# Row factors carried to all partitions by DMA in ten of sixteen graphs, an ELU without a GpSimd pass, and loads split over two queues

## The chip, the core and the metric

The kernel runs on one core of one Trainium2 chip. What counts is the device time of one execution in microseconds. Before the change it is 1097.34 us (median of 3 runs, 1097.25 to 1097.4).

## The reference

Sixteen graphs of 512 nodes with 128 features share one adjacency matrix. Four layers follow each other. Each adds its result to its input and normalises the rows (mean and variance over 128 features).

```python
# x: (16, 512, 128), adj: (512, 512)
# layer 0: 4 heads of 32
scores = where(adj == 0, -inf, q @ k.T / sqrt(32));  o = softmax(scores) @ v
x = layernorm(x + o @ wo.T + bo)
# layer 1: one head
e = leaky_relu(s1[:, None] + s2[None, :], 0.2);  a = softmax(masked e);  x = layernorm(x + a @ (x @ W))
# layer 2: 8 heads of 16, the same kind of scores, a prior of adj, then @ W_out.T
# layer 3
r = relu(x @ w1 + b1)                                  # 256 wide
z = elu(elu(softmax(leaky scores, unmasked) @ (r @ W_fc))) + r
r = relu(z @ w2 + b2)                                  # 128 wide
y = relu(elu(elu(softmax(masked leaky scores) @ (r @ W_hand))) + r)
x = layernorm(x + y)
```

A leaky score of a source i and a target j makes exp(leaky(s_i + d_j)), which is the larger of two products of a factor of i and a factor of j. So the kernel needs, for each target tile, the 512 source factors as a row that stands on all 128 partitions, and the two target factors as one number per partition.

## The kernel before, in words

The nodes of a graph stand as 4 chunks (`C`) of 128 partitions. Every engine works through its own written-out list of stages (`ORDER`, read by `turns`), two characters for each entry: the stage's letter and the graph. Part k of a stage is its k-th appearance. The lists interleave the layers of several graphs, up to four at a time. Which of the eight PSUM banks a stage uses is a list too (`BANK_OF_USE`). All engines, and SyncE's list of DMAs too, work strictly in this order, and semaphores tie them together.

The stages that the change touches:

- **Row factors of layers 1, 3 and 3b** (3b is the second attention of layer 3). ScalarE makes `R`, 128x4, one source factor per node (`exps`). TensorE transposes each column, broadcast to 128 wide, into a bank (`spread_sources`, L569, 4 instructions), and VectorE reads the bank four times: `masked_weights` (L1114) for layers 1 and 3b, `weights` (L1130) for layer 3.
- **Layer 0's reciprocals.** `l0_rcp` makes 128x16 reciprocals; `l0_rd` (L531, 16 matmuls of 32 columns of weights) spreads them into a bank, each head on its 32 partitions; `l0_o` (L1044) multiplies.
- **Layer 2's rows** go by DMA already, in all graphs. VectorE transposes 32x32 blocks of `R2` (`l2_turn`, L1194), SyncE writes them to a line in HBM with 4 DMAs (`l2_rows`, L432) and reads each head's line back with a broadcast to 128 partitions (`l2_spread`, L439) into one of five buffers `row`. VectorE reads a row four times (`l2_p`, L1207).
- **ELU.** After the attention of layer 3, ScalarE writes the quotient v (`l3_v`, L847); GpSimd makes min(v, 0) in pieces of 128x128 (`below_zero`, L1370); ScalarE takes exp twice (L864, L870), and VectorE puts the result together (L1238, L1249). The same holds for 3b (L856).
- **The start.** SyncE issues nine DMAs of projections, then adj as one transfer (L399), then all the later weights (`late_loads`), then x of graph 0 (L423). TensorE runs 12 matmuls that nobody reads (`WARM_UP`, L453), turns five weights (L457, L458) and goes on with x.
- **Fillers.** An entry Z (`keep_warm`, L697) is two matmuls that nobody reads, written into the bank of the next stage. There are 102 of them, 204 matmuls; each fp32 matmul is two instructions in the trace.

## Time and profile before

| | us |
|---|---|
| median of 3 runs | 1097.34 |
| the profiled execution | 1097.66 |
| its span | 1095.9 |
| TensorE busy (PE) | 1028.9 |
| VectorE busy (DVE) | 925.4 |
| ScalarE busy (ACT) | 727.9 |
| GpSimd busy (POOL) | 376.2 |

The span is the profiled execution from its first to its last instruction, and lies 1.8 us below that execution's own time. Busy time is the union of an engine's instructions, so a group's busy time divided by its count is less than the mean duration of one of them, since they overlap in the pipeline. PEld is the loading of weights into TensorE, beside its matmuls. The page's rows for the engines give shares of the span; the stretches further down show where in the span an engine is full.

### The profile page before, as it was taken

What the parts mean: (1) busy time and instruction counts of PE and PEld (TensorE: products, weight loads), DVE (VectorE), ACT (ScalarE), POOL (GpSimd) and SP (SyncE); (2) the same over time, 40 slices, a digit from 0 to 9 for tenths busy, and PEclk for the clock granted to TensorE, in tenths of its full rate; (3) what the DMA queues carried; (4) which work ended last, traced back from release to release, by engine and by line L of the source; (5) the groups of instructions that cost most, each with busy time, mean ns of one, the idle gap of its engine ahead of it and who ended that gap; (6) DMA issues with size and microseconds to landing.
All of it is one profiled execution on the core that took longest, in us unless ns stands there. A gap on an engine that the chain in (4) does not pass through costs nothing. (4 is left out here: it accounts for less than half of the span.)

```text
span 1095.9 us, 26875 instructions
## 1 busy us (share of the span) xinstructions
PE 1028.9 (94%) x9253; PEld 770.6 (70%) x9253; DVE 925.4 (84%) x2533; ACT 727.9 (66%) x1901; POOL 376.2 (34%) x781
## 2 busy tenths in 40 slices
PE   4899989999999999999999999999999999889895
PEld 3576657777777776867777777768677778576785
DVE  2757999999899989899998999998999988877342
ACT  1797776766767777786767677777867663543522
POOL 1013413432525243343325252443433264341322
PEclk6999999999999999999999999999999999999999
DMA  5001110202020210102020201102020202020000
GB/s 125 2 11 60 54 56 20 70 20 78 22 69 21 69 32 32 58 21 79 21 76 23 69 21 65 35 30 60 21 79 11 78 13 68 12 78 20 10 1 20
DMA packets 30997, 46.82 MB, mean 43 GB/s; under 512 B 7824, under 2 KB 10128, under 8 KB 30736
## 3 DMA queue, kind: packets, MB, share of 16 engines
q1 hardware_dynamic: 30864, 45.11, 13.2%
q8 instruction: 76, 1.25, 0.5%
q14 instruction: 57, 0.47, 0.1%
HBM read 40.64 MB, written 4.46 MB: 41 GB/s over the span
## 5 line engine op out<-in xcount | busy, mean ns | idle before, releaser
L1207 DVE SCALAR_TENSOR_TENSOR P<-row,t2e,mask_t 128x512 f32<-128x512 f32 x512 | 358.6, 761 | 7.9 <-PE bank L605 7.0
L751 ACT ACTIVATE probs<-probs,neg_max 128x512 f32<-128x512 f32 x256 | 186.1, 729 | 16.6 <-DVE neg_max L1024 15.9
L1016 DVE CUSTOM_DVE_ANT_0 probs<-bank,mask_add 128x512 f32<-128x512 f32 x256 | 168.0, 682 | 28.7 <-PE bank L502 28.3
L761 ACT ACTIVATE probs_t<-bank 128x512 f32<-128x512 f32 x256 | 151.2, 620 | 4.5 <-PE bank L510 4.2
L510 PE MATMUL bank<-ident,probs 128*128 128x128 f32 x1024 | 144.0, 277 | 7.4 <-ACT probs L751 6.3
L510 PEld LDWEIGHTS bank<-ident,probs 128*128 128x128 f32 x1024 | 113.8, 141 | 36.9 <-ACT probs L751 25.1
L796 ACT ACTIVATE x<-x,shift_l,rstd_l 128x128 f32<-128x128 f32 x256 | 105.0, 484 | 44.7 <-POOL shift_l L1343 44.7
L1361 POOL TENSOR_TENSOR t<-t 128x128 f32<-128x128 f32 x128 | 48.7, 412 | 204.3 <-ACT t L788 204.3
L605 PE MATMUL bank<-P,GH 128*32 128x512 f32 x1024 | 116.2, 594 | 1.9 <-DVE P L1207 1.2
L650 PE MATMUL bank<-t,l_P 128*128 128x257 f32 x512 | 115.1, 383 | 1.1 <-DVE l_P L1130 1.1
L1370 POOL TENSOR_SCALAR e<-v 128x128 f32<-128x128 f32 x128 | 74.8, 611 | 113.6 <-ACT v L847 113.6
L650 PEld LDWEIGHTS bank<-t,l_P 128*128 128x128 f32 x512 | 95.9, 190 | 16.4 <-issue 2.2
L1328 POOL TENSOR_TENSOR rstd_l<-mv_l,ln_eps 128x4 f32<-128x4 f32 x64 | 16.5, 258 | 192.7 <-DVE mv_l L1070 192.6
L605 PEld LDWEIGHTS bank<-P,GH 128*32 128x32 f32 x1024 | 31.2, 110 | 68.2 <-issue 66.3
L1336 POOL TENSOR_TENSOR rstd_l<-rstd_l,neg_half 128x4 f32<-128x4 f32 x64 | 75.0, 1173 | 3.0
L1320 POOL TENSOR_TENSOR x_in<-x_in,bias_o 128x128 f32<-128x128 f32 x64 | 30.3, 505 | 132.9 <-PE bank L473 132.9
L502 PE MATMUL bank<-head_k,head_q 32*128 32x512 f32 x512 | 72.4, 638 | 1.8 <-DVE l_P L1114 0.9
L521 PE MATMUL bank<-probs_t,v 128*32 128x128 f32 x2048 | 70.0, 278 | 0.9 <-ACT probs_t L761 0.7
L521 PEld LDWEIGHTS bank<-probs_t,v 128*32 128x32 f32 x2048 | 52.6, 110 | 19.8 <-issue 12.0
L733 ACT ACTIVATE xTl<-bank 128x512 f32<-128x512 f32 x64 | 38.1, 595 | 40.6 <-PE bank L473 40.4
L581 PE MATMUL bank<-t,l3b_P 128*128 128x129 f32 x512 | 62.3, 277 | 0.5 <-DVE l3b_P L1114 0.5
L581 PE MATMUL bank<-t,l_P 128*128 128x129 f32 x512 | 61.1, 278 | 0.0
(168 smaller groups left out, 2016.3 us busy)
## 6 DMA issues: line engine op xcount, KB each, us to landing
row<-line SPq DMA_DIRECT2D x128, 256.0 KB, 3.5
x_in<-in_x SPq DMA_DIRECT2D x16, 256.0 KB, 2.6
out<-x SPq DMA_DIRECT2D x16, 256.0 KB, 2.1
l_P<-in_adj SPq DMA_DIRECT2D x1, 1024.0 KB, 7.5
line<-turned SPq DMA_DIRECT2D x64, 4.0 KB, 1.4
w_fc<-in_L_gnn_W_fc SPq DMA_DIRECT2D x1, 256.0 KB, 3.0
P<-in_L_gnn_a_fc SPq DMA_DIRECT2D x1, 256.0 KB, 3.6
w_cat<-in_L_gnn_W SPq DMA_DIRECT2D x2, 64.0 KB, 5.9
```

What stands on the lines that cost most here:

```text
L510: last = pe.transpose(ps[:, j * P:(j + 1) * P], probs[m // HEADS0 % 2][:, m % HEADS0, j * P:(j + 1) * P], ident[:, :])
L521: last = pe.matmul(ps[DH0 * h:DH0 * (h + 1), 0:P], g.of(v0)[:, j, DH0 * h:DH0 * (h + 1)], probs_t[c % 2][:, h, j, :], start=(j == 0), stop ...
L581: last = pe.matmul(ps[:, c * (D + 1):(c + 1) * (D + 1)], gat[n]["P"][:, j, (2 * k + c) * P:(2 * k + c + 1) * P], g.of(t)[:, j, 2:3 + D], s ...
L605: last = pe.matmul(ps[DH0 * h:DH0 * (h + 1), :], g.of(GH)[:, j, (GROUP2 * q + h) * W2:(GROUP2 * q + h) * W2 + DH0], P2[:, h, j, :], start= ...
L650: last = pe.matmul(ps[:, 0:HID + 1], gat["l3"]["P"][:, j, c * P:(c + 1) * P], g.of(t3)[:, j, 2:3 + HID], start=(j == 0), stop=(j == C - 1))
L751: act.activation(e, e, ACT.Exp, bias=neg_max[:, m:m + 1], scale=SCALE0, accum_out=g.of(den0)[:, m:m + 1])\
L761: act.activation(probs_t[c % 2][:, h, :, :].rearrange("p j n -> p (j n)"), ps("l0_t", g, m)[:, :], ACT.Copy)\
L796: last = act.activation(y[:, c, :], y[:, c, :], ACT.Identity, bias=shift[n][:, c:c + 1], scale=rstd[n][:, c:c + 1])
L1016: dve.tensor_tensor_reduce(probs[c % 2][:, h, :], ps("l0_s", g, m)[:, :], mask_add[:, c, :], 1.0, -3.0e38, ALU.add, ALU.max, row_max[:, m: ...
L1207: last = dve.scalar_tensor_tensor(P2[:, h % GROUP2, j, :], row(g, h)[:, :], g.of(t2e)[:, j, h:h + 1], mask_t[:, j, :], ALU.max, ALU.mult)
L1336: pool.tensor_tensor(rstd[n][:, :], rstd[n][:, :], neg_half[:, :], ALU.pow)\
L1370: last = pool.tensor_scalar(e[:, c, q:q + P], v(g)[:, c, q:q + P], 0.0, None, ALU.min)
```

## The change

1. **Rows by DMA in graphs 2 to 11** (`ROWS_BY_DMA = range(2, 12)`). For layers 1, 3 and 3b the four columns of `R` are turned on VectorE (`turn`), written to HBM with one DMA (`lay_out`) and read back with a broadcast (`spread`) into a `row` buffer, from which VectorE reads them. Layer 0's reciprocals go the same way (`l0_spread`). In the other six graphs TensorE spreads them as before. Layer 2's lines are written with one DMA where it was four. There are six row buffers where there were five, and which transfer goes to which buffer is a list (`ROW_OF_USE`).
2. **The companion.** A column of ones stands beside the features, and gives the softmax's sum. Beside it now stands a column of its negative, so that the reciprocal yields 1/sum and -1/sum (258 columns for 257, 130 for 129). ScalarE reads the bank twice: v = o/sum, and e = relu(-o/sum). The first exp takes scale -1. GpSimd's pass is gone.
3. **Loads.** ScalarE's queue issues wq, wk, both biases, wv and bias_v; SyncE issues adj in four transfers, the first at once, then x of graph 0, then the later weights. wo, w_out and bias_o come later and are turned later (`out_T`). `WARM_UP` is 4.
4. All lists are written anew. Fillers: 82, that is 164 matmuls.

The core of the diff, long lists left out:

```diff
-ROWS = 5
+ROWS = 6
-WARM_UP = 12
+WARM_UP = 4
+ROWS_BY_DMA = range(2, 12)
 ...
+            def lay_out(n, turned):
+                def f(g, k):
+                    sp.wait_ge(*(sig if n == "l2" else dma_sig)(n + "_turned", g, 1))
 ...
+                    sp.dma_start(g.of(line[n]).rearrange("r (q s) -> q r s", s=BLOCK),
+                                 turned[:, :]).then_inc(signal[n + "_rows"], 16)
+            def free_row(stage, g, k):
+                r, _, last = row_use[stage, k, g.i]
+                if last:
+                    sp.wait_ge(*row_read(last[0], last[2], last[1]))
+                return rows[r], row_filled[r]
+            def spread(n):
+                def f(g, k):
+                    if k == 0:
+                        sp.wait_ge(*(sig if n == "l2" else dma_sig)(n + "_rows", g, 16))
+                    to, done = free_row(n + "_spread", g, k)
+                    sp.dma_start(to[:, :], g.of(line[n])[k * C:(k + 1) * C, :].rearrange("c p -> (c p)")
+                                 .rearrange("(o n) -> o n", o=1).broadcast_to([P, N_NODES])).then_inc(done, 16)
 ...
-                    made = dve.tensor_scalar(q["P"][:, j, :], ps(n + "_s", g)[:, :], q["g"][:, j:j + 1], q["b"][:, j:j + 1],
+                    made = dve.tensor_scalar(q["P"][:, j, :], sources(n, g), q["g"][:, j:j + 1], q["b"][:, j:j + 1],
 ...
+                o, q = ps("l3_o", g, c)[:, 0:HID], gat["l3"]["rden"]
+                act.activation(v3[:, c, :], o, ACT.Copy, scale=q[:, c, 0:1])
+                act.activation(e3[:, c, :], o, ACT.Relu, scale=q[:, c, 1:2]).then_inc(emptied("l3_o", g, c), 1)
```

**Three places in the lists.** On SyncE at the start, before: the projections are first, and x of graph 0 comes after all of the late loads.

```order
L393 DMA bias_q<-in_L0_gnn_bq 128x1
L394 DMA bias_k<-in_L0_gnn_bk 128x1
L395 DMA bias_v<-in_L0_gnn_bv 128x128
L396 DMA bias_o<-in_L0_gnn_bo 128x128
L399 DMA l1_P<-in_adj 128x2048
L403 DMA w1_cat<-in_L1_gnn_W 128x128
L404 DMA P2<-in_L1_gnn_a 128x256
```

After, on the same engine, ahead of and behind the late loads:

```order
L441 DMA l1_P<-in_adj 128x512
L465 DMA x_in_0<-in_x 128x512
L445 DMA w1_cat<-in_L1_gnn_W 128x128
L446 DMA P2<-in_L1_gnn_a 128x256
...
L460 DMA P2<-in_L3_gnn_a_hand 128x256
L441 DMA l1_P<-in_adj 128x512
L465 DMA x_in_1<-in_x 128x512
L435 DMA l3b_P<-in_L0_gnn_wo 128x128
```

x of graph 0 moved from behind the late loads to second place; the second quarter of adj stands behind them.

On SyncE around layer 2 of graph 3, before: a line is written in four pieces and its heads follow one another.

```order
L423 DMA x_in_0<-in_x 128x512
L432 DMA line2_1<-turned2 32x32 x4
L439 DMA row2<-line2_0 128x512
L439 DMA row3<-line2_1 128x512
L439 DMA row4<-line2_1 128x512
L439 DMA row0<-line2_1 128x512
```

After, in the same region: lines and rows of layer 0 and layer 1 of other graphs stand between the heads of layer 2.

```order
L465 DMA x_in_0<-in_x 128x512
L476 DMA l2_line1<-turned2 4x32x32
L491 DMA row3<-l2_line1 128x512
L476 DMA l0_line1<-turned0 4x32x32
L498 DMA row1<-l0_line1 128x1x512
L491 DMA row0<-l2_line1 128x512
L491 DMA row4<-l2_line1 128x512
L476 DMA l1_line0<-l1_turned 4x32x32
L491 DMA row2<-l1_line0 128x512
```

A transfer of one layer now waits in the same queue behind the waits of another layer.

On TensorE at the very end, before: the last graph's layer 3 and 3b with the fillers between them.

```order
L697 MATMUL bank<-ones,ident 128x128 x32
L659 MATMUL bank<-ident,v 128x128 x8
L697 MATMUL bank<-ones,ident 128x128 x2
L674 MATMUL bank<-ident,out_t 128x128 x4
L667 MATMUL bank<-h_t,w3b 128x512 x2
...
L697 MATMUL bank<-ones,ident 128x128 x12
L581 MATMUL bank<-t_0,l3b_P 128x129 x16
L697 MATMUL bank<-ones,ident 128x128 x26
L674 MATMUL bank<-ident,out_t 128x128 x4
```

After, the same stages:

```order
L771 MATMUL bank<-ones,ident 128x128 x14
L732 MATMUL bank<-ident,v 128x128 x8
L747 MATMUL bank<-ident,out_t 128x128 x4
L740 MATMUL bank<-h_t,w3b 128x512 x2
...
L771 MATMUL bank<-ones,ident 128x128 x12
L654 MATMUL bank<-t_0,l3b_P 128x130 x16
L771 MATMUL bank<-ones,ident 128x128 x14
L747 MATMUL bank<-ident,out_t 128x128 x4
```

Behind the last attention product of layer 0 the list of before has 192 filler matmuls, that of after 108.

## Rows read from the trace of the kernel before

**Rows 1.** The page, part 1: busy us (share) and instructions of each engine.
```profile
PE 1028.9 (94%) x9253; PEld 770.6 (70%) x9253; DVE 925.4 (84%) x2533; ACT 727.9 (66%) x1901; POOL 376.2 (34%) x781
```
**Rows 2.** Stretches: length, then busy us of PE, PEld, DVE, ACT, POOL; PEclk, DMA.
```profile
300.00:400.00 100.00, 99.24 (x911) 75.53 (x910) 93.36 (x250) 74.40 (x201) 35.34 (x76) 1.00 0.15 49
...
1060.00:1080.00 20.00, 17.37 (x134) 15.10 (x134) 9.45 (x23) 7.47 (x16) 5.25 (x13) 1.00 0.04 14
```
**Rows 3.** Timeline of SyncE's queue: start us, us; loads of x, seven periods apart.
```profile
346.98 0.33 SPq L423 DMA_DIRECT2D x_in<-in_x  x1
...
769.42 0.33 SPq L423 DMA_DIRECT2D x_in<-in_x  x1
```
**Rows 4.** Groups by line, TensorE: busy us, mean ns, idle before.
```profile
L650 PE MATMUL bank<-t,l_P 128*128 128x257 f32 x512 | 115.1, 383 | 1.1 <-DVE l_P L1130 1.1
...
L697 PE MATMUL bank<-ones,ident 128*128 128x128 f32 x408 | 50.0, 275 | 1.5 <-ACT head_q L741 0.8 <-ACT mask_t L718 0.7
...
L569 PE MATMUL bank<-ident,l_R 128*128 128x128 f32 x128 | 19.7, 279 | 1.1 <-ACT l_g L788 0.9
...
L531 PE MATMUL bank<-ident,rden 128*32 128x128 f32 x512 | 16.9, 273 | 0.0
```
**Rows 5.** Timeline of the start: start us, us, engine.
```profile
4.47 0.43 SPq L396 DMA_DIRECT2D bias_o<-in_L_gnn_bo  x1
...
10.00 1.12 PE L457 MATMUL bank<-ident,l3b_P 128*128 128x128 f32 x4 [3.26 <-DMA bias_o<-in_L_gnn_bo]
...
15.66 0.91 SPq L423 DMA_DIRECT2D x_in<-in_x  x2
...
20.20 1.09 PE L473 MATMUL bank<-ident,x_in 128*128 128x128 f32 x4 [8.87 <-DMA x_in<-in_x]
21.33 0.60 ACT L733 ACTIVATE xTl<-bank 128x512 f32<-128x512 f32 x1 [8.94 <-PE bank L473]
...
29.04 0.69 DVE L1016 CUSTOM_DVE_ANT_0 probs<-bank,mask_add 128x512 f32<-128x512 f32 x1
```
**Rows 6.** Timeline of the end: ELU of the last graph.
```profile
1055.52 0.47 ACT L847 ACTIVATE v<-bank,l_rden 128x256 f32<-128x256 f32 x1 [1.26 <-DVE l_rden L1233]
1056.27 3.96 POOL L1370 TENSOR_SCALAR e<-v 128x128 f32<-128x128 f32 x8 [13.43 <-ACT v L847]
...
1060.26 1.06 ACT L864 ACTIVATE e<-e 128x1024 f32<-128x1024 f32 x1 [2.33 <-POOL e L1370]
...
1081.00 0.62 ACT L856 ACTIVATE x<-bank,l3b_rden 128x128 f32<-128x128 f32 x2 [1.16 <-DVE l3b_rden L1141]
1081.77 2.00 POOL L1370 TENSOR_SCALAR e<-x 128x128 f32<-128x128 f32 x4 [6.89 <-issue]
1083.81 0.63 ACT L864 ACTIVATE e<-e 128x512 f32<-128x512 f32 x1 [2.18 <-POOL e L1370]
```
**Rows 7.** Groups by line, VectorE.
```profile
L1207 DVE SCALAR_TENSOR_TENSOR P<-row,t2e,mask_t 128x512 f32<-128x512 f32 x512 | 358.6, 761 | 7.9 <-PE bank L605 7.0 <-DMA row<-line 0.2
...
L1130 DVE TENSOR_SCALAR l_P<-bank,l_g,l_b 128x512 f32<-128x512 f32 x64 | 50.7, 795 | 0.1
...
L1114 DVE SCALAR_TENSOR_TENSOR l_P<-bank,l_b,mask_t 128x512 f32<-128x512 f32 x64 | 46.4, 739 | 2.0 <-PE bank L569 2.0
...
L1194 DVE STREAM_TRANSPOSE turned<-R 128x32 f32<-128x32 f32 x16 | 3.2, 199 | 0.0
...
L941 DVE TENSOR_SCALAR l_P<-l_P 128x512 f32<-128x512 int32 x4 | 2.2, 609 | 0.0
```
**Rows 8.** Timeline of VectorE and SyncE's queue: graph 0's layer 2 rows.
```profile
100.11 0.21 DVE L1194 STREAM_TRANSPOSE turned<-R 128x32 f32<-128x32 f32 x1
...
100.35 1.74 SPq L432 DMA_DIRECT2D line<-turned  x4
...
103.11 6.63 SPq L439 DMA_DIRECT2D row<-line  x6
...
106.66 2.73 DVE L1207 SCALAR_TENSOR_TENSOR P<-row,t2e,mask_t 128x512 f32<-128x512 f32 x4
```

More of the change, by code:

```diff
@@ L205, in bank_uses, with row_uses @@
     return used
+def row_uses():
+    used, transfers, last, at = {}, [0] * ROWS, [None] * ROWS, 0
+    for name, g, k in turns("sp"):
+        if name.endswith("_spread"):
+            r = int(ROW_OF_USE[at])
+            at += 1
+            transfers[r] += 1
+            used[name, k, g.i] = r, transfers[r], last[r]
+            last[r] = name, k, g
+    return used
 def build_program(nc, x, adj, w, out):
     use = bank_uses()
+    row_use = row_uses()
     with ExitStack() as ctx:
@@ L321, in build_program @@
         for n in GATS:
-            for what, k in (("c4", 1), ("dd", 2), ("b", 3)):
+            for what, k in (("c4", 1), ("dd", 2), ("b", 3), ("turned", 1), ("p", 1)):
                 sem(f"{n}_{what}", k)
@@ L326, in build_program @@
         for n in ("l3", "l3b"):
-            for what in ("min", "ea", "eb"):
+            for what in ("ea", "eb"):
                 sem(f"{n}_{what}", 1)
@@ L360, in empty, with by_dma, dma_sig, sources_read @@
             return bank[b]
-        def row(g, h):
-            return rows[(HEADS2 * g.i + h) % ROWS]
-        def row_done(g, h):
-            n = HEADS2 * g.i + h
-            return row_filled[n % ROWS], 16 * (n // ROWS + 1)
-        line2 = [nc.dram_tensor(f"line2_{q}", [HEADS2 * C, P], F32, kind="Internal").ap() for q in range(2)]
+        def by_dma(g, back=0):
+            return g.i - back in ROWS_BY_DMA
+        def dma_sig(name, g, k=1, back=0):
+            return signal[name], per_graph[name] * ROWS_BY_DMA.index(g.i - back) + k
+        def sources_read(n, g, back=0):
+            return dma_sig(n + "_p", g, 1, back) if by_dma(g, back) else took(n + "_s", g, 0, back)
+        def divided(g, back=0):
+            return dma_sig("o0_made", g, 1, back) if by_dma(g, back) else took("l0_rd", g, 0, back)
+        def row(stage, g, k=0):
+            return rows[row_use[stage, k, g.i][0]]
+        def spread_done(stage, g, k=0):
+            r, transfers, _ = row_use[stage, k, g.i]
+            return row_filled[r], 16 * transfers
+        def row_read(stage, g, k):
+            if stage == "l2_spread":
+                return sig("p2_made", g, k + 1)
+            return divided(g) if stage == "l0_spread" else sources_read(stage[:-len("_spread")], g)
+        line = {n: [nc.dram_tensor(f"{n}_line{q}", [BLOCK, P], F32, kind="Internal").ap() for q in range(2)]
+                for n in ("l0", "l1", "l2", "l3", "l3b")}
         x_v = x.rearrange("b (p c) d -> b p c d", c=C)
@@ L486, in l0_v @@
                 pe.wait_ge(*took("l0_xT", g))
+                if g.i == 0:
+                    pe.wait_ge(*took("proj_T", g))
                 ps = empty("l0_v", g)
@@ L535, in l0_y @@
             def l0_y(g, k):
-                pe.wait_ge(*took("l0_rd", g))
+                pe.wait_ge(*divided(g))
+                if g.i == 0:
+                    pe.wait_ge(*took("out_T", g))
                 ps = empty("l0_y", g)
@@ L766, in l0_ov @@
                 if g.has(1):
-                    act.wait_ge(*took("l0_rd", g, back=1))
+                    act.wait_ge(*divided(g, back=1))
                 act.activation(o0_raw[:, c * P:(c + 1) * P], ps("l0_pv", g, c)[:, 0:P], ACT.Copy)\
@@ new lines, in l3b_v @@
+            def l3b_v(g, k):
+                act.wait_ge(*sig("l3b_rden", g, k + 1))
+                if g.has(2):
+                    act.wait_ge(g.of(stored), 16 * (g.i // 2))
+                if g.has(1):
+                    act.wait_ge(*sig("z4_made", g, 1, back=1))
+                for c in range(2):
+                    i, q = 2 * k + c, gat["l3b"]["rden"]
+                    o = ps("l3b_o", g, k)[:, c * (D + 2):c * (D + 2) + D]
+                    act.activation(g.of(x4)[:, i, :], o, ACT.Copy, scale=q[:, i, 0:1])
+                    last = act.activation(e4[:, i, :], o, ACT.Relu, scale=q[:, i, 1:2])
+                last.then_inc(emptied("l3b_o", g, k), 1)
@@ L865, in elu_first @@
+            def elu_first(n, e, parts):
+                def f(g, k):
+                    for c in range(parts):
+                        act.wait_ge(*took(n + "_o", g, c))
+                    act.activation(e[:, :, :], e[:, :, :], ACT.Exp, scale=-1.0).then_inc(signal[n + "_ea"], 1)
                 return f
@@ L1102, in scores, with sources @@
                 return f
+            def sources(n, g):
+                return row(n + "_spread", g)[:, :] if by_dma(g) else ps(n + "_s", g)[:, :]
             def masked_weights(n):
@@ L1303, in _ @@
             pool.memset(ln_eps[:, :], LN_EPS)
+            for t in [rden0] + [gat[n]["R"] for n in GATS]:
+                pool.memset(t[:, :], 0.0)
             for t in GH:
```

488 lines of the change are left out of this document (248 added, 240 removed), and 16 rows, old and new, of the table STAGES.

## Prediction

> **What bounds the kernel now.** I read the page's shares first: TensorE 94%, VectorE 84% [rows 1]. These are means over three different parts, so I went on to the stretches. In the middle TensorE is busy 99.2 of 100 us and VectorE 93.4 [rows 2]; the lists repeat there, and the loads of x give the period: from 346.98 to 769.42 is 422.4 us for seven graphs, 60.3 us each [rows 3]. By the same shares a period holds 0.992 x 60.3 = 59.9 us of TensorE and 56.3 us of VectorE. So TensorE is the bound, and VectorE would be next, only 3.6 us away. The other two parts are bound by latency: the start, where TensorE waits for x until 20.20 us and the first scores are read at 29.04 us [rows 5], and the end, where in 20 us VectorE is busy 9.45 [rows 2] and much of what TensorE does are fillers.
>
> **The change part by part.** Terms are against the profiled span, 1095.9 us.
>
> *TensorE's spreads, graphs 2 to 11.* `l0_rd` is 32 instructions in a graph at 16.9/512 = 0.033 us, so 1.06 us; a spread of four transposes is 4 x 19.7/128 = 0.62 us, and there are three [rows 4]. Together 2.9 us a graph, 29 us for ten. This is the upper end: busy times of short groups include the overlap with their neighbours. For the lower end I use the rate at which back-to-back 128-column instructions go. The fillers, 50.0/408 = 0.123 us each [rows 4], make a spread 0.49, and three of them 1.5; `l0_rd` runs four narrow matmuls beside each other, 8 groups of them, so about 8 x 0.123 = 1.0. That is 2.5 a graph, 25 us. The lower end is the nearer, as the stages stand between others with no gap: **-24**, with a further half a microsecond for what overlaps. The companion's column costs 1/257 of layer 3's 115.1 us [rows 4], 0.45, and 3b, with as many instructions, the same again: +0.9. Net **-23**, bounds -28 and -21.
>
> *What takes their place on VectorE.* 40 block transposes at 0.199 = 8.0 us; 80 readings of a row where it was a bank, at 761 for 739 ns, 1.8 us [rows 7]. The 40 readings of layer 3's `weights` take 795 ns from a bank. No row shows this form from SBUF with fp32; the nearest is L941 (int32 in SBUF, with a stride), 609 ns [rows 7]. I take it, 40 x 0.186 = -7.4; bounds: nothing gained, and twice the row's gain, -15. The sum is +2.4 us, 0.24 a graph. VectorE's 56.3 becomes 56.5 in a period that TensorE alone would make 60.3 - 2.3 = 58.0: busy 97.5%, where it was 93.4%. That is close enough to cost something.
>
> The trace shows 795 ns for fp32 from PSUM. The Trainium skill, VectorE: DVE Perf Modes (Mode 2×_2P — use both read ports for one tensor) says that a one-source fp32 instruction with source and destination in SBUF yields two results a cycle, and none from PSUM. No row of before tests it on this form. By it L1240 would take roughly half of 795 ns, an estimate, the VectorE sum would be -6 us and its share about 96%. The forecast doesn't rest on this.
>
> *The way of a row.* From the end of the transposing (100.32) to the first reading of the row (106.66) it takes 6.3 us [rows 8], of which 1.74 is the issue of four DMAs; with one, about 1.3 less, 5.0 us. TensorE's way is 0.62 plus a semaphore. Whether this is seen depends on what VectorE has in its list between `turn` and the reading. Adding up the durations of what stands there in the new list, by the rows of before, I find for the 40 relays 4 to 17 us; five are below 5.0, by 1 us at most. Layer 2's rows go this way already, and VectorE waited for them for 0.2 us in all [rows 7]. The waits in the queue (a head of layer 2 waits behind a line of layer 0 that isn't turned yet) come on top. For VectorE's crowding and the relays together: **+5**; bounds 0 and +20 (the second is the rival below).
>
> *The start.* Today: the nine projections' last load lands at 10.0 us, x is issued at 15.66 behind all else and its transposes start at 20.20; from the copy of xT (21.33) to the first scores read (29.04) it is 7.7 us, of which 1.1 are transposes of the mask that now stand elsewhere [rows 5]. After: six projection loads on ScalarE's queue are issued in 6 x 0.47 = 2.8 us and land, with the 5.5 us between the issue and landing of bias_o [rows 5] as the long end and half of that as the short, between 6 and 9 us. x, issued second, is there by then. Turning and copying three weights needs some 2 us, then 6.6: the first scores are read at 15 to 17 us. The second quarter of adj is issued behind the late loads at about 12 us and is needed three microseconds after the first scores, so it hardly shows. **-14**; bounds -9 and -17.
>
> *The end.* Layer 3: ScalarE's last v is done at 1055.99, and exp starts at 1060.26, since GpSimd needs 3.96 us for eight pieces [rows 6]. With the companion, one more copy of 0.47 us stands between: 3.8 us less. 3b: from 1081.62 to 1083.81 becomes about 0.7 us: 1.5 less. So 5.3 us a graph, where latency counts. The layers 3 of four graphs (12 to 15) lie behind layer 0's end, 21 us. They are partly beside each other, and the relays aren't there to help or hurt (graphs 12 to 15 go by TensorE). The lists show the same from another side: behind layer 0's last product there are 84 filler matmuls fewer, at 50.0/204 = 0.245 us each [rows 4], 21 us. I take **-19**; bounds -8 (fillers shrink, but other waits come instead) and -26. In the middle a shorter ELU is worth nothing, since TensorE is full. ScalarE gets 64 copies of 0.47 and 64 of about 0.3, 50 us over the whole; it is at 74 of 100 in the middle [rows 2] and goes to about 80, hidden.
>
> *Sum.* 1095.9 - 23 + 5 - 14 - 19 = 1044.9 us of span. The profiled execution took 1.8 more than its span and the median is 0.3 below it: **1046 us**, 51 less than before. The start's fillers (28 matmuls more ahead of layer 0's end) lie in waits there.
>
> **The rivals.**
>
> *A. VectorE becomes the bound.* For: 97.5% is asked of it, and the stretch of before had 93.4; the new lists don't repeat from graph to graph, so there are more places where the two meet badly. Against: where TensorE was the bound, VectorE's gaps were simply what was left. If it gives 95%, a third of the way between, a period is 56.5/0.95 = 59.5 us, and 1.5 of the 2.3 us are lost: 1046 + 15 - 5 + some unhidden relays of 5 = 1061.
>
> *B. The start doesn't shift what follows.* Layer 0 of graphs 0 and 1 is a chain of ScalarE, VectorE and TensorE; if it is held by the quarters of adj, or by wo and w_out whose turning stands early in TensorE's list, some 9 of the 14 us are lost: 1055.
>
> *C. More comes than I count.* The stages of the end fit better as TensorE and VectorE both have fewer waits, reading SBUF gains twice the row, and the spreads are worth 2.9: 23 -> 28, +5 -> 0, 19 -> 25: 1030.
>
> *D. Slower than before: the single queue.* SyncE's list is strictly in order, and it now holds 12 row transfers a graph with five lines. Each relay that comes late holds VectorE, and behind VectorE the next turn, so lateness feeds itself. The price of one relay fully on the path is the 5.0 us. The gain of 51 is used up when the 40 relays cost 1.3 us each beyond the 5 I have put in. With half of them fully on the path, 20 x 5.0 = 100: 1146. Against it: SyncE's queue was nearly always waiting for others, six buffers for twelve rows give each about 25 us, and the distances in the list are at the length of the way or above it.
>
> **How the numbers follow.** Forecast 0.50, A 0.19, B 0.13, C 0.13, D 0.05. The forecast's own range is 1038 to 1053. The 8-in-10 range takes in A and B and most of C: 1032 to 1066. A measurement of this kernel tells 0.2%, 2.2 us, from no change. Faster by over 0.2%: 0.95; within it: 0.01; slower: 0.04, nearly all of D.
>
> **What the profile after would show.** Loads of x between 300 and 700 us on average 57.5 to 59 us apart (near 59.5 or above: A). First reading of scores at 15 to 17 us. TensorE busy near 994 us (1028.9 less 23 and less 48 idle matmuls); VectorE 920 to 930, and idle before its readings of rows for DMA under 5 us in all. L1240 from a row between 400 and 800 ns, to be read by form. At the end, exp of layer 3 within 1.2 us of ScalarE's last copy. GpSimd about 16 x 6.0 = 95 us less [rows 6], 281. I would be wrong in the mechanism if TensorE were under 96% busy in the middle and waited there for VectorE, or if the gain lay in one of the three parts alone.

## The result, and the profile after

The kernel after takes 1093.29 us (median of 20, 1089.04 to 1097.35) where the kernel before takes 1097.01 (also 20 runs). The ratio is 0.9969, interval 0.9958 to 0.9981: about 4 us less. Forecast were 1046, with 1032 to 1066 as the range. The direction was right, and 47 of the 51 us did not come. In what follows one of the ten runs of `elu_alone`, which took 1322.16 us at a mean granted clock of 0.746, is left out of the ratios; all others lie within 0.5% of their kernel's median.

The page's part 1 of the profiled execution (span 1091.6 us, its own time 1093.39), beside [rows 1]:

```profile
PE 1007.3 (92%) x8717; PEld 737.6 (68%) x8717; DVE 912.2 (84%) x2573; ACT 766.9 (70%) x2029; POOL 303.9 (28%) x610
```

TensorE's busy time fell by 21.6 us, yet its idle time rose from 1095.9 - 1028.9 = 67.0 to 84.3 us, by 17.3. What was taken from TensorE came back as waiting. Two stretches of the middle show it, where [rows 2] had 99.24 and 93.36:

```profile
300.00:400.00 100.00, 94.56 (x907) 68.84 (x906) 81.65 (x256) 75.77 (x211) 30.19 (x66) 1.00 0.20 56
...
500.00:600.00 100.00, 93.20 (x794) 67.46 (x792) 86.64 (x255) 77.40 (x209) 38.00 (x66) 1.00 0.22 71
```

TensorE **and** VectorE are both less busy here. It isn't so in every stretch (VectorE has 94.86 from 400 to 500 us, as before), but over the 600 us from 200 to 800 TensorE goes from 98.9% to 94.6% and VectorE from 93.8% to 90.0%. Neither is nearer to full than it was. Two loads of x, five apart, give the period, as [rows 3] did:

```profile
331.75 0.33 SPq L465 DMA_DIRECT2D x_in<-in_x  x1
...
634.34 0.34 SPq L465 DMA_DIRECT2D x_in<-in_x  x1
```

302.6 us for five graphs are 60.5 each: no shorter than the 60.3 of before. TensorE's groups that answer to [rows 4]:

```profile
L723 PE MATMUL bank<-t,l_P 128*128 128x258 f32 x512 | 119.5, 384 | 1.3 <-DVE l_P L1240 1.1
...
L771 PE MATMUL bank<-ones,ident 128*128 128x128 f32 x328 | 42.4, 280 | 2.2 <-ACT x L941 1.7 <-DVE row_max L1108 0.6
...
L642 PE MATMUL bank<-ident,l_R 128*128 128x128 f32 x48 | 7.3, 276 | 0.7 <-ACT l_g L873 0.7
...
L642 PE MATMUL bank<-ident,l3b_R 128*128 128x128 f32 x24 | 3.8, 282 | 0.4 <-ACT t L873 0.3
...
L602 PE MATMUL bank<-ident,rden 128*32 128x128 f32 x192 | 6.3, 273 | 0.0
```

The row of 3b in before, which [rows 4] doesn't have:

```profile
L569 PE MATMUL bank<-ident,l3b_R 128*128 128x128 f32 x64 | 9.8, 275 | 0.5 <-ACT t L788 0.4
```

The instructions went as planned: against [rows 4] 80 transposes fewer for rows of layers 1 and 3 and 40 fewer for 3b, 320 narrow matmuls fewer for layer 0, 80 filler instructions (40 matmuls) fewer. These three groups of spreads fell by 12.4, 6.0 and 10.6 us, 29.0 together; the product of layer 3 with its companion rose by 4.4. The start, beside [rows 5]:

```profile
5.80 1.06 PE L540 MATMUL bank<-ident,x_in 128*128 128x128 f32 x4
6.89 0.60 ACT L818 ACTIVATE xTl<-bank 128x512 f32<-128x512 f32 x1 [1.91 <-PE bank L540]
...
8.96 0.55 PE L524 MATMUL bank<-ident,l3b_P 128*128 128x128 f32 x3 [2.10 <-DMA bias_v<-in_L_gnn_bv]
...
15.93 0.69 DVE L1108 CUSTOM_DVE_ANT_0 probs<-bank,mask_add 128x512 f32<-128x512 f32 x1 [0.36 <-PE bank L573]
```

The first scores are read 13.1 us earlier. The end, the ELU of layer 3 in the last graph, beside [rows 6]:

```profile
1057.30 0.47 ACT L933 ACTIVATE v<-bank,l_rden 128x256 f32<-128x256 f32 x1 [0.90 <-DVE l_rden L1337]
1057.67 0.47 ACT L934 ACTIVATE e<-bank,l_rden 128x256 f32<-128x256 f32 x1
1058.25 1.06 ACT L963 ACTIVATE e<-e 128x1024 f32<-128x1024 f32 x1
```

The exponential starts 0.11 us behind the last copy, where it was 4.3 behind. Yet the stretch from the last copy of layer 0's values to the end of the span went from 212.1 us (883.8 to 1095.9) only to 209.0 (882.6 to 1091.6). The copy, before and after:

```profile
883.79 0.28 ACT L768 ACTIVATE o_raw<-bank 128x128 f32<-128x128 f32 x1 [0.57 <-PE bank L521]
```
```profile
882.64 0.28 ACT L853 ACTIVATE o_raw<-bank 128x128 f32<-128x128 f32 x1 [0.71 <-PE bank L592]
```

VectorE's groups, beside [rows 7]:

```profile
L1224 DVE SCALAR_TENSOR_TENSOR l3b_P<-row,l3b_b,mask_t 128x512 f32<-128x512 f32 x40 | 30.6, 767 | 1.8 <-issue 1.1 <-DMA row<-l3b_line 0.6
L1224 DVE SCALAR_TENSOR_TENSOR l_P<-row,l_b,mask_t 128x512 f32<-128x512 f32 x40 | 29.4, 735 | 0.5 <-issue 0.5
...
L1240 DVE TENSOR_SCALAR l_P<-row,l_g,l_b 128x512 f32<-128x512 f32 x40 | 21.6, 548 | 2.1 <-DMA row<-l_line 1.4 <-issue 0.6
...
L1240 DVE TENSOR_SCALAR l_P<-bank,l_g,l_b 128x512 f32<-128x512 f32 x24 | 18.7, 794 | 1.7 <-issue 1.3 <-PE bank L642 0.3
```

And VectorE's waits (us in total, times, longest):

```profile
DVE probs L1108 <- PE bank L573: 20.0, 18, 3.6
...
DVE o_t L1149 <- DMA row<-l_line: 9.0, 4, 3.0
```

With the waits for rows at L1311, L1240 and L1224 (2.3, 1.4, 0.6) that is 13.3 us for rows, where [rows 7] had 0.2. ScalarE's waits moved too. Before, its normalisations waited 44.7 us for `shift_l` and its exponentials 15.9 us for `neg_max`; now

```profile
ACT x L881 <- POOL shift_l L1457: 58.6, 31, 6.1
...
ACT probs L836 <- DVE neg_max L1116: 33.4, 22, 4.4
```

### The profile page after: what moved, and what is told of

It reads as the page before. It is cut to its first block, busy times and chain, and to the rows that moved or that the text cites. A ratio compares the mean times of both kernels' runs of the same rounds, so it can differ in the third digit from the quotient of the medians.

```text
span 1091.6 us, 25883 instructions
## 1 busy us (share of the span) xinstructions
PE 1007.3 (92%) x8717; PEld 737.6 (68%) x8717; DVE 912.2 (84%) x2573; ACT 766.9 (70%) x2029; POOL 303.9 (28%) x610
## 4 chain that ended last, share of the span: by engine, by line
PE 21%; DVE 15%; issue 6%; ACT 5%; POOL 4%; DMA 3%; SPq 0%; DVEq 0%; ACTq 0%; POOLq 0%
DVE P L1311 6%; PE bank L678 3%; PE bank L723 3%; DVE l3b_P L1224 2%; PE bank L714 2%; ACT x L881 2%; POOL rstd_l L1450 2%; PE bank L654 2%; PE bank L581 2%; PE bank L740 1%; PE bank L624 1%; PE bank L592 1%; DMA row<-l_line 1%; DVE stats_l L1167 1%; PE bank L702 1%
## 5 line engine op out<-in xcount | busy, mean ns | idle before, releaser
L1311 DVE SCALAR_TENSOR_TENSOR P<-row,t2e,mask_t 128x512 f32<-128x512 f32 x512 | 359.9, 762 | 11.2 <-PE bank L678 8.9
L881 ACT ACTIVATE x<-x,shift_l,rstd_l 128x128 f32<-128x128 f32 x256 | 105.1, 488 | 58.7 <-POOL shift_l L1457 58.6
L1442 POOL TENSOR_TENSOR rstd_l<-mv_l,ln_eps 128x4 f32<-128x4 f32 x64 | 22.9, 358 | 354.7 <-DVE mv_l L1177 354.7
L723 PE MATMUL bank<-t,l_P 128*128 128x258 f32 x512 | 119.5, 384 | 1.3 <-DVE l_P L1240 1.1
L1475 POOL TENSOR_TENSOR t<-t 128x128 f32<-128x128 f32 x128 | 64.7, 535 | 186.2 <-ACT t L873 186.1
L1450 POOL TENSOR_TENSOR rstd_l<-rstd_l,neg_half 128x4 f32<-128x4 f32 x64 | 71.8, 1124 | 4.4
L654 PE MATMUL bank<-t,l3b_P 128*128 128x130 f32 x512 | 61.8, 277 | 3.2 <-DVE l3b_P L1224 3.1
L654 PEld LDWEIGHTS bank<-t,l3b_P 128*128 128x128 f32 x512 | 59.2, 191 | 5.5 <-DVE l3b_P L1224 4.3
L714 PE MATMUL bank<-w_fc,h_t 128*128 128x258 f32 x256 | 62.1, 391 | 0.4 <-issue 0.4
L1467 POOL TENSOR_TENSOR x<-x 128x128 f32<-128x128 f32 x64 | 38.4, 629 | 83.7 <-issue 61.8
L654 PE MATMUL bank<-t,l_P 128*128 128x129 f32 x512 | 60.5, 276 | 0.4 <-DVE l_P L1224 0.4
```

What stands on the lines that cost most here:

```text
L654: last = pe.matmul(ps[:, c * width:(c + 1) * width], gat[n]["P"][:, j, (2 * k + c) * P:(2 * k + c + 1) * P], g.of(t)[:, j, 2:2 + width], s ...
L714: last = pe.matmul(ps[:, 0:2 + HID], h3_t[:, q, c * P:(c + 1) * P], w3_fc[:, q, :], start=(q == 0), stop=(q == 1))
L723: last = pe.matmul(ps[:, 0:HID + 2], gat["l3"]["P"][:, j, c * P:(c + 1) * P], g.of(t3)[:, j, 2:4 + HID], start=(j == 0), stop=(j == C - 1))
L881: last = act.activation(y[:, c, :], y[:, c, :], ACT.Identity, bias=shift[n][:, c:c + 1], scale=rstd[n][:, c:c + 1])
L1311: last = dve.scalar_tensor_tensor(P2[:, h % GROUP2, j, :], row("l2_spread", g, h)[:, :], g.of(t2e)[:, j, h:h + 1], mask_t[:, j, :], ALU.ma ...
L1450: pool.tensor_tensor(rstd[n][:, :], rstd[n][:, :], neg_half[:, :], ALU.pow)\
```

## The experiments

Gains below are (1 - ratio) x 1097 us, with the interval of the ratio to the kernel before. The kernel after itself stands at 0.9969, 3.4 us by this reckoning. The cuts below leave work out: the columns, chunks and rows that are not made keep other numbers, so these kernels don't compute the reference and serve for their time alone. "Given lists" are the lists that a kernel came with.

### Two parts of the change in given lists

**rows_fixed**: the kernel after without the way of the 40 rows. Their line and row transfers and the waits for them are left out, and VectorE reads a part of `w3_fc` in SBUF instead.

```diff
+        fixed_row = w3_fc[:, :, :].rearrange("p a b -> p (a b)")[:, 0:N_NODES]
...
-            return rows[row_use[stage, k, g.i][0]]
+            return rows[row_use[stage, k, g.i][0]] if stage == "l2_spread" else fixed_row
```

> The kernel after, but in graphs 2 to 11 VectorE reads a part of w3_fc that stands in SBUF instead of the 40 rows of layers 0, 1, 3 and 3b; their 40 line transfers and 40 row transfers are left out (so the weights of these layers are other numbers), the 40 transposes on VectorE stay, and so do all lists. Theory 'relays' (the way of a row and SyncE's one queue ate the gain: waits for rows of 13 us are in the trace after, and what they push behind them): the time falls by 25 us or more from 1093, to 1055 to 1068. Theory 'order' (the new lists let the engines wait for each other, whatever the rows do): 1085 to 1093, at most the 8 us that are worth most of the waits for rows.

1080.79 us, 0.9836 (0.9815 to 0.9857). Against after: 14.6 us less, about the 13.3 us of waits for rows and no more. The theory "relays" wanted 25 or more, and "order" at most 8, so the result lies between the two. The ways of the rows cost three times the 5 us forecast, and still explain only 10 of the 47 missing. How much of the 14.6 other lists would hide without any change to the rows, the relisted kernels below show.

**elu_alone**: the companion ELU in the kernel before (the core of the edit; GpSimd's minima and their entries in its list are gone too).

```diff
-                act.activation(v3[:, c, :], ps("l3_o", g, c)[:, 0:HID], ACT.Copy, scale=gat["l3"]["rden"][:, c:c + 1])\
+                act.activation(v3[:, c, :], o, ACT.Copy, scale=q[:, c, 0:1])
+                act.activation(e3[:, c, :], o, ACT.Relu, scale=q[:, c, 1:2]).then_inc(emptied("l3_o", g, c), 1)
```

> The kernel before with the companion ELU alone: GpSimd's 192 minima go, the value product of layers 3 and 3b carries one column more, ScalarE makes a second, clipped copy of 128 results (2.4 us a graph by 477 and 376 ns less what is hidden), lists otherwise unchanged. By the prediction's terms: +1 for the columns, -5 for the ELU behind the last product, so 1093. If ScalarE is close to the bound, as theory 'order' has it (it must meet VectorE and TensorE in a fixed order and each microsecond on it pushes the others), the 38 us more of ScalarE cost 5 to 15 us in the middle: 1098 to 1107. If the relief of GpSimd (107 us less) helps the normalisations, below 1088.

1101.28 us, 1.0031 (1.0019 to 1.0042): slower by 3.4. A part that was to take work off the path at the end, and to give ScalarE 2.4 us a graph "hidden", costs time in lists that were made for another amount.

### Who binds: the same cut on each engine

**vector_less_before, vector_less_after**: 3 us a graph less of VectorE.

```diff
+                n = N_NODES if g.i == 0 else 416
                 for j in range(C):
-                    last = dve.scalar_tensor_tensor(P2[:, h % GROUP2, j, :], row(g, h)[:, :], g.of(t2e)[:, j, h:h + 1],
+                    last = dve.scalar_tensor_tensor(P2[:, h % GROUP2, j, 0:n], row(g, h)[:, 0:n], g.of(t2e)[:, j, h:h + 1],
...
```

> The kernel after, with VectorE's 512-column weights of layer 2 made over 416 columns in graphs 1 to 15 (the rest keeps the last graph's numbers): about 0.10 us less for each of 480 instructions, 48 us less of VectorE, the rest unchanged. Prediction's view (TensorE bounds, VectorE follows): 1083 to 1090. Theory 'VectorE bounds or shares the bound': -30 to -48, so 1045 to 1063.

> The kernel before with the same cut of VectorE: 416 columns for the weights of layer 2 in graphs 1 to 15, 48 us less of VectorE. Prediction's view (TensorE 99 per cent busy in the middle): -2 to -12, so 1085 to 1095. If VectorE had shared the bound already before the change: 1060 to 1075.

**tensor_less_before, tensor_less_after**: 2 to 3 us a graph less of TensorE.

```diff
...
-                pe.matmul(ps[:, :], w3a[:, k * P:(k + 1) * P], xT["l3"][:, :], start=True, stop=True)\
+                n = N_NODES if g.i == 0 else 384
+                pe.matmul(ps[:, 0:n], w3a[:, k * P:(k + 1) * P], xT["l3"][:, 0:n], start=True, stop=True)\
...
-                for j in range(C):
+                parts = C if g.i == 0 else C - 1
+                for j in range(parts):
...
```

q, k and the second product of the mlp are cut to 384 columns in the same way.

> The kernel after with less work for TensorE in graphs 1 to 15: the value product of layer 3 over 3 of its 4 chunks (1.8 us a graph), q, k and both products of the mlp over 384 of 512 columns (1.3 us a graph), in all 47 us; the rest of the columns keeps old numbers, everything else unchanged. If TensorE still bounds: -35 to -47, 1046 to 1058. If the three engines wait for each other and none bounds alone: -10 to -25, like the -19 of the same size of cut on VectorE, 1068 to 1083. If VectorE bounds: -10 or less.

> The kernel before with the same 47 us less on TensorE. If TensorE bounds it, as its 98.6 to 99.2 per cent say: -30 to -47, 1050 to 1067. If VectorE's 93 per cent take over at once: -10 to -25, 1072 to 1087. With the first, the prediction's reading of before was right and the new lists or relays are at fault; with the second, cutting TensorE by 24 us could never have given 24 us.

**scalar_less_before, scalar_less_after**: 2.5 us a graph less of ScalarE (`n = N_NODES if g.i == 0 else 336` in three copies), and **both_less_before, both_less_after**: the cuts of VectorE and TensorE together.

> The kernel after with 22 of ScalarE's copies of 512 columns a graph (probabilities transposed, the four turned inputs, the mlp's first layer) over 336 columns in graphs 1 to 15: by 606 ns for 512 columns and 293 for 128, 0.14 us each, 47 us in all; the columns left out keep old numbers. ScalarE is 72 to 78 per cent busy. If busy shares tell who bounds: -5 at most, 1088 to 1093. If a chain of waits through all engines bounds: -10 to -22, 1071 to 1083, as much as VectorE's cut or more than TensorE's.

> The kernel before with the same cut of ScalarE. If busy shares tell who bounds (TensorE 99 per cent): -3 at most, 1094 to 1097. If the chain goes through all engines here as well: -8 to -15, 1082 to 1089, and then an addition to ScalarE (the clipped copies of the change) costs in both kernels.

> The kernel before with both cuts at once, 48 us less of VectorE (weights of layer 2 over 416 columns) and 47 us less of TensorE (value product of layer 3 over 3 chunks of 4, q, k and mlp over 384 columns), graphs 1 to 15; the columns left out keep old numbers. Alone they gave -12 and -10. If the two engines bound in turn (each hides the cut of the other): clearly more than the sum, -32 to -45, so 1053 to 1066. If each acts on its own share of one chain that goes from engine to engine: about the sum, -22, 1072 to 1079.

> The kernel after with the same two cuts; alone they gave -19 (VectorE) and -6 (TensorE). Bounds in turn: 1048 to 1060. One chain from engine to engine: about the sum, 1065 to 1072.

| cut | busy time taken (before / after) | before: median, ratio (interval), gain | after: median, ratio (interval), gain against after |
|---|---|---|---|
| VectorE | 46.6 / 43.5 us | 1085.63, 0.9888 (0.9873-0.9904), 12.3 | 1074.38, 0.9784 (0.9764-0.9805), 20.3 |
| TensorE | 34.3 / 31.0 | 1087.67, 0.9915 (0.9898-0.9931), 9.3 | 1087.53, 0.9908 (0.9892-0.9923), 6.7 |
| ScalarE | 37.0 / 36.2 | 1087.42, 0.9910 (0.9895-0.9925), 9.9 | 1091.72, 0.9948 (0.9933-0.9963), 2.3 |
| VectorE and TensorE | 90.5 / 90.6 | 1063.38, 0.9698 (0.9682-0.9714), 33.1 | 1058.73, 0.9656 (0.9639-0.9673), 34.3 |

In the kernel before, where TensorE is 99% busy, a microsecond less of busy time on TensorE gives 0.27 us, the same as on VectorE (0.26) or ScalarE (0.27, at 74% busy). The figure is rough: the interval of TensorE's gain (7.6 to 11.2 us) alone makes it 0.22 to 0.33, and the same cut took 42.2 us of busy time off TensorE when VectorE's went with it, but 34.3 alone. Both cuts together give 33.1, half again the sum of 21.6, and per microsecond of busy time 0.37. So in before the engines bind in turn: each waits for the others at many places of a fixed order, and relief on one meets the other soon.

The kernel after is another case. There VectorE's cut gives 0.47, TensorE's 0.22 and ScalarE's 0.06, and both together (0.38) hardly more than the sum (27.0 of 34.3 us, 0.36). VectorE counts most in it, as rival A had it, though its share of the middle fell. The cuts were made without new lists, so they tell what an engine's time is worth in a given order, not what it would be worth in lists made for it.

Some expectations were missed. VectorE's cut in after (1074.38) fell between its two ranges. TensorE's in before (1087.67) lay above both of its ranges, the upper one by less than 1 us, and in after it met only "if VectorE bounds, -10 or less". ScalarE's met the chain through all engines in before and the busy shares in after, so neither of the two theories has both.

Back to before. The middle of tensor_less_before, with a granted clock of 1.00 from 200 to 850 us, shows what the busy share hides. A stretch, and the loads of x of [rows 3]:

```profile
300.00:400.00 100.00, 96.20 (x945) 73.85 (x947) 94.48 (x257) 74.26 (x198) 36.83 (x76) 1.00 0.15 49
```
```profile
344.50 0.33 SPq L423 DMA_DIRECT2D x_in<-in_x  x1
...
763.18 0.33 SPq L423 DMA_DIRECT2D x_in<-in_x  x1
```

418.7 us for seven graphs, 59.8 each: 0.5 us shorter for 2.3 us (34.3/15) less work, and TensorE falls to 96%. With both cuts the same two loads are 410.7 us apart, 58.7 each. The Trainium skill, Perfetto Trace Analysis (Identifying the Most-Contended Engine), warns of just this: the busy share of matmuls says little on how near TensorE is to its limit, since they are pipelined, and the share of weight loads should be taken instead. The trace agrees: 99.24 of matmuls stood beside 75.53 of weight loads [rows 2]. The whole span of tensor_less_before also has a lower granted clock behind the middle (0.97 from 850 to 900 us, 0.93 from 900 to 950, where before has 1.00), which may take some of its gain; the period in the middle is free of that, and gives 0.22 us per us.

### The same instructions in other lists

**relist_after, relist_before** and their second seeds: nothing but the tables changes. A search moved entries within each engine's list and swapped banks and row buffers, so that each engine should find its operands earlier; a seed is a starting point of its random choices. The first line of SyncE's list and that of TensorE's banks in relist_after:

```diff
     "sp":
-        "00a01000a1300000a2a3f0g0g0g0g0b2c2g0g0g0g0a4d2f1e2g1g1g1g1b3c3g1g1a5g1g1d3f2e3g2g2g2g2b4g2c4g2g2g2a6"
+        "3000a0000010a100a2a3f0g0g0g0g0b2c2g0g0g0g0a4f1d2g1e2g1g1b3c3g1g1g1a5g1g1d3e3f2g2g2g2g2b4g2c4g2g2g2f3"
...
 BANK_OF_USE = (
-    "01234567012345670157210635635467325710327510243751602453761024563170246532146750321546031254670321547603271504"
+    "16130265143072652701345162051372064753041520763412705731465132407536412516235162376526461532703751406164037526"
```

> The kernel after with every instruction kept and only ORDER, BANK_OF_USE and ROW_OF_USE changed: the same entries in another order on all five engines, found by a search that moves entries and swaps banks and rows so that each engine finds its operands earlier. Theory 'order' (the change is worth what was predicted, its new lists lose it): 1040 to 1065, at least 30 us under the 1093 of the lists that came with the change. Theory 'mechanism' (relays, clipped copies and contention cost what the spreads saved, in whatever order): no lower than the kernel before with lists found in the same way, so the two relisted kernels within 5 us.

> The kernel before with its ORDER and BANK_OF_USE found anew by the same search, every instruction kept. TensorE is 98.6 to 99.2 per cent busy in the middle, so what can be found lies in the start, the end and short stalls inside the busy stretches: 1065 to 1090. The distance to relist_after is the worth of the change with lists of one making: by theory 'order' 15 to 40 us, by theory 'mechanism' -5 to 5.

> relist_after again from another seed of the search: every instruction of the kernel after, another order. If the search scatters little, within 5 us of 1065.4; then the distance of 22 us to the relisted kernel before is the change's and not the luck of one list.

> relist_before again from another seed: within 5 us of 1087.5 if the search scatters little. If it falls below 1075, the two relisted kernels can't be told apart by this method.

**relist_elu**: elu_alone, relisted. **relist_no_relays**: the kernel after with all spreads on TensorE, relisted.

```diff
-ROWS_BY_DMA = range(2, 12)
+ROWS_BY_DMA = range(0, 0)
```

> The kernel before with the companion ELU alone (elu_alone) and lists found by the same search. Against relist_before (1087.5) it is the worth of the ELU: by the prediction's terms +0.9 for the column and the ELU's part of the end, some -10: 1077 to 1080; if the clipped copies on ScalarE cost what they did in the old lists, +3 to +4: 1088 to 1092. Its distance to relist_no_relays is the worth of the new loads: by the prediction 14.

> The kernel after with ROWS_BY_DMA empty, so all rows and reciprocals are spread by TensorE as before, while the loads and the ELU are the new ones; lists and banks found by the same search. Its distance to relist_after (1065.4) is the worth of the relays. If TensorE's saved time counts a fifth to a quarter, as its cut did alone, less what the rows' ways cost: within 5 us of relist_after. If it counts as predicted (-23 + 5): 1080 to 1086.

| lists found by the search | median us | ratio (interval) |
|---|---|---|
| before, two seeds | 1087.49, 1090.66 | 0.9913 (0.9896-0.9930), 0.9929 (0.9911-0.9947) |
| before with the ELU | 1079.02 | 0.9827 (0.9810-0.9843) |
| with ELU and new loads, no relays | 1068.98 | 0.9734 (0.9720-0.9749) |
| all of after, two seeds | 1065.36, 1058.49 | 0.9708 (0.9693-0.9723), 0.9640 (0.9625-0.9654) |

The theory "order" (the change is worth what it should, its lists lose it) held in direction: without one instruction changed, the kernel after gains 28.6 (at least 30 were expected) and 36.1 us, the kernel before 9.5 and 7.8. With lists of one making the change is worth 0.9921 - 0.9674 = 0.0247, 27 us (means of two seeds; 22 from the nearest pair of seeds, 32 from the farthest): 10 for the ELU, 10 for the loads, 7 for the relays. The seeds of after differ by 7.5 us (5 were expected), so the relays' 7 is not told from nothing, and the 10 of each of the others, from kernels with one seed, may be off by several us. Down the table (without before's second seed, 886.1) the last copy of layer 0's values starts at 882.5, 880.3, 867.1, and 861.0 and 851.9 us: the gain of the loads now does reach the middle's end.

The stretch behind that copy tells as much. It takes 201.8 us (203.7 with the second seed) in before relisted, 197.0 with the ELU, 201.1 with ELU and loads, and 203.8 and 204.1 in all of after. So the ELU alone shortens the end by 5 to 7 us, and the whole change doesn't shorten it at all, in lists of one making either. All of its 27 us lie ahead of layer 0's end, where the copy comes 28 us earlier (means of two seeds; one trace each).

**relist_best** (longer search, against durations that vary more) and **relist_best_tensor_less** (the cut of TensorE in it):

> The kernel after, every instruction kept, lists searched longer than in relist_after and relist_after_2 and against durations that vary more from one instruction to the next (GpSimd's and the transfers' above all), so that the order doesn't rest on one exact timing. 1045 to 1058; above 1058.5 the longer search has brought nothing that the chip shows.

> relist_best with the cut of tensor_less_after (some 31 us of TensorE's busy time in graphs 1 to 15; the columns and the chunk left out keep old numbers). In the lists of before and after it gave 9.9 and 6.7 us, 0.29 and 0.2 us per us. If the fraction is a matter of the lists, and TensorE is what is left to bind once others wait less: 15 us or more. If it is the same 0.2 to 0.3: 5 to 10 us, and TensorE's time is worth no more in good lists.

relist_best takes 1051.08 us, 0.9570 (0.9549 to 0.9591): 46 us under before and 42 under after by the medians (in ratio 0.9570/0.9969 = 0.960), with after's instructions. Before was not given this longer search, so the 46 us are not the worth of the change. Its page, two stretches, and the wait that had shown in after:

```profile
PE 1001.5 (95%) x8717; PEld 734.0 (70%) x8717; DVE 919.6 (88%) x2573; ACT 768.1 (73%) x2029; POOL 326.6 (31%) x610
```
```profile
300.00:400.00 100.00, 99.37 (x926) 75.09 (x918) 92.41 (x269) 82.53 (x221) 38.43 (x70) 1.00 0.20 62
...
600.00:700.00 100.00, 97.02 (x844) 70.78 (x843) 96.46 (x272) 72.89 (x195) 38.18 (x66) 1.00 0.22 68
```
```profile
DVE o_t L1149 <- DMA row<-l_line: 0.5, 1, 0.5
```

TensorE's idle time is 1048.8 - 1001.5 = 47.3 us (84.3 in after), VectorE's waits for rows are 0.5 us (13.3), and the loads of x from 219.00 to 739.61 are 57.8 us apart on average, in the forecast's 57.5 to 59. The rows travel the same way; the list only has other work in front of their reading. The cut gives 1039.45, 0.9466 (0.9450 to 0.9482), 11.4 us for 38.3 us of busy time: 0.30. So even in these lists a microsecond of TensorE is worth a third of one. That is under the "15 or more" and above the "5 to 10" of the expectation.

## Why the prediction was wrong, by its own steps

**"So TensorE is the bound" failed**, and with it the weight of every term. The working took 99.2% busy as proof that a period is as long as TensorE's work. The cut shows 0.27 us per us. By the rows of the groups the work left out is 29.0 us of spreads (forecast 25 to 29) less 4.4 for the companion (forecast 0.9), so about the 23 of the sum; at 0.27 that is worth 6. In lists of one making the relays bring 3 and 10 us (the two seeds of after against relist_no_relays), where the terms -23 and +5 promised 18. The term -23 was rightly sized as work and about four times too large as time. That TensorE's whole busy time fell by 21.6 us is not a second proof of the size: it should have fallen by 35, to 994, with the fillers and warm-up matmuls that are gone too (10.3 us by their rows). The other groups, instructions unchanged, hold the 13 us more; why is open.

**The lists were read for one thing only.** The step on the way of a row compared the distance from `turn` to reading with 5.0 us and found the lists good enough. It took for granted that they were otherwise as good as before's. They are not: the search finds 32 us in after's (mean of two seeds), 9 in before's. These 24 us are half of the miss of 47. The other half is that with lists of one making the change is worth 27 us, not 51. That the new lists are uneven is not the fault: loads of x are 41.6 to 77.4 us apart in after between 228.91 and 773.03, and 42.4 to 75.4 apart in relist_best, from 219.00 to 739.61, which is 42 us faster. What the trace of after shows without experiment is that TensorE and VectorE are both less busy in the middle, while ScalarE's share is up by one or two points only (75.77, [rows 2] 74.40; from 200 to 800 us 75.6% for 73.6%).

**Relays, +5**: 14.6 in these lists (rows_fixed). These are not to be added to the 24 us of the lists: after relisting VectorE waits hardly at all for rows (3.0 and 0.9 us, 0.5 in relist_best). The way was taken as 5.0 us. The second longest wait at `o_t` shows what it is for layer 0 (a turn at 319.14 ahead of it):

```profile
321.12 2.73 DVE L1311 SCALAR_TENSOR_TENSOR P<-row,t2e,mask_t 128x512 f32<-128x512 f32 x4
321.31 0.55 SPq L498 DMA_DIRECT2D row<-l_line  x1
321.92 0.95 SPq L491 DMA_DIRECT2D row<-l_line  x2
...
326.96 0.69 DVE L1149 TENSOR_TENSOR o_t<-row,o_raw 128x512 f32<-128x512 f32 x1 [2.44 <-DMA row<-l_line]
```

2.2 us to the issue of the row and 5.6 from there to its use, 7.8 in all; other rows are issued at the same time. In relist_best a relay of layer 0 in the same region takes 7.9:

```profile
303.95 0.20 DVE L1139 STREAM_TRANSPOSE turned<-rden 128x32 f32<-128x32 f32 x1
...
306.17 0.55 SPq L498 DMA_DIRECT2D row<-l_line  x1
...
311.83 0.69 DVE L1149 TENSOR_TENSOR o_t<-row,o_raw 128x512 f32<-128x512 f32 x1 [0.51 <-DMA row<-l_line]
```

There 7.4 us of other work stand between, in after 5.4 (7.8 less the wait). Rival D named this mechanism with 100 us; its place was right, its size wrong, and the kernel was not slower than before.

**The start, -14**: the first scores came at 15.93, within the 15 to 17. But layer 0's last value copy moved from 883.8 to 882.6 only: the 13 us were given back along the way. That is rival B's result without its mechanism, which was a chain in the first two graphs: the first copy of layer 2's values (graph 0) still comes 12.1 us earlier, at 119.5 for 131.6. In relisted kernels the loads bring 10: 13.2 at layer 0's end (880.3 to 867.1), 4 of which are lost behind it. (The list has 44 filler matmuls more ahead of layer 0's end, not the 28 that the sum names; 28 are its entries there.)

**The end, -19**: the exponential followed its copy at once, as said, yet the stretch behind layer 0 shrank by 3.1 us. The inference from 84 fillers fewer was unsound: a filler's absence doesn't say that the wait around it is gone. This term, of all, did not come in relisted kernels either (203.8 and 204.1 us for 201.8 and 203.7). The ELU, 3.4 us slower in old lists and 10 faster in new ones, does shorten the end by 5 to 7 us where it stands alone; which part of the rest takes that back was not tried. "74 of 100 goes to about 80, hidden" was wrong in before, where ScalarE's time counts 0.27 per us; in after it counts 0.06.

**Rival A** had the right suspicion (two engines that meet badly, VectorE's time counting most: 0.47) with a price from VectorE's busy share alone. That 95% was not reached in after (94.86 at most in a stretch of 100 us), while the fast relist_best has 95.6 to 96.5 from 500 to 800 us. So a high share of VectorE is not what made after slow.

Sizes that held: the spreads' work on TensorE; L1240 from a row 548 ns (609 taken, 400 to 800 forecast). VectorE's busy time came out lower, 912.2 for 920 to 930, and GpSimd's higher, 303.9 for 281 (270.6 in elu_alone). The named sign of being wrong in the mechanism, TensorE under 96% busy in the middle, came true (94.6% from 200 to 800 us); its second half, that TensorE waits there for VectorE, did in part: of its waits in these 600 us VectorE ended 12 us, ScalarE 16 and a load of x 3, and VectorE was less busy too.

By ratio, 27 us of the change's worth less the 24 us by which its lists are worse are the 3 to 4 measured. This is true by how the two are reckoned and proves nothing more. Which entries of the lists make up the 24 was not tried.

## What to carry to other kernels

A busy share of 99% doesn't make an engine the bound: cut its work by a few per cent in a trial, and the others' too, and count each saving with the measured fraction, which holds for the order it was measured in. Where the order of work is a table, a change is work plus order; compare both kernels with lists of one making before judging the work. A wait that a change brings may be cured by moving other work in front of it, without making it shorter.

## What the runs showed of the hardware

- **From a row in SBUF a one-source instruction gains, a two-source one doesn't.** L1240 went from 794 ns to 548 (448 to 807), while L1224 stayed at 735 and 767 where the bank took 733 to 735. The Trainium skill, VectorE: DVE Perf Modes (Mode 2×_2P), says that a one-source fp32 instruction between tiles in SBUF yields two results a cycle; by that, as an estimate, roughly half of 795 was due. The trace agrees in direction only: the mean is 0.69 of it, the shortest 448.
- **A short GpSimd instruction (L1442) takes 202 ns at the median and up to 1216.** Its mean rose from 258 ns to 358. In one place where it and its followers are long, VectorE's weights stand beside them:

```profile
405.01 0.62 POOL L1442 TENSOR_TENSOR rstd_l<-mv_l,ln_eps 128x4 f32<-128x4 f32 x1 [4.47 <-DVE mv_l L1177]
405.06 0.47 ACT L934 ACTIVATE e<-bank,l_rden 128x256 f32<-128x256 f32 x1
405.49 2.73 DVE L1311 SCALAR_TENSOR_TENSOR P<-row,t2e,mask_t 128x512 f32<-128x512 f32 x4
405.58 0.70 POOL L1443 TENSOR_TENSOR shift_l<-mv_l,neg_one 128x4 f32<-128x4 f32 x1
406.37 1.40 POOL L1450 TENSOR_TENSOR rstd_l<-rstd_l,neg_half 128x4 f32<-128x4 f32 x1
407.85 0.43 POOL L1457 TENSOR_TENSOR shift_l<-shift_l,rstd_l 128x4 f32<-128x4 f32 x1
...
408.22 0.73 DVE L1224 SCALAR_TENSOR_TENSOR l3b_P<-row,l3b_b,mask_t 128x512 f32<-128x512 f32 x1
408.31 0.49 ACT L881 ACTIVATE x<-x,shift_l,rstd_l 128x128 f32<-128x128 f32 x1 [2.78 <-POOL shift_l L1457]
```

  Four instructions on 128x4 numbers take 3.3 us here, and ScalarE stands idle for 2.8. The Trainium skill, SBUF — State Buffer (SBUF: two separate sides), says that a VectorE instruction with two SBUF inputs and a GpSimd one that reads SBUF exclude each other. The row fits that, and the change gives 80 of VectorE's instructions a second SBUF input where they had a bank. But that these made the mean rise is not shown, and other runs speak against it as the only cause. The same instruction takes 349 ns in relist_before and 365 in relist_elu, which have none of the 80, and 271 in relist_no_relays, which has none either. The row of relist_before:

```profile
L1328 POOL TENSOR_TENSOR rstd_l<-mv_l,ln_eps 128x4 f32<-128x4 f32 x64 | 22.3, 349 | 153.4 <-DVE mv_l L1070 153.1
```

  The order of work alone is enough to raise it. The transfers are not the reason: rows_fixed, without them, has 361. And relist_best, with 369, is 42 us faster than after.
- **With a cut in TensorE's work its granted clock was a little lower.** 1.00 is 2.4 GHz, and a figure below it means that a part of the stretch ran at 1.2. The four runs of tensor_less_before have means of 0.979 to 0.984, the seven of before beside them 0.985 to 0.988. From 900 to 950 us before has 1.00, and tensor_less_before, where TensorE had also been less busy ahead of it (45.95 of 50 us, clock 0.97, for 47.86), has 0.93:

```profile
900.00:950.00 50.00, 45.48 (x323) 35.43 (x322) 40.71 (x98) 25.13 (x67) 19.87 (x37) 1.00 0.14 49
```
```profile
900.00:950.00 50.00, 44.05 (x309) 34.96 (x305) 40.77 (x99) 20.32 (x52) 19.86 (x36) 0.93 0.14 44
```

  A stretch that is less busy doesn't always have the lower clock. tensor_less_after has less and 1.00:

```profile
900.00:950.00 50.00, 41.06 (x292) 33.72 (x295) 42.11 (x116) 30.93 (x83) 17.80 (x35) 1.00 0.18 54
```
